# A recurrence's values spread by DMA, its key products on GpSimd, weights issued behind the first inputs

## What is computed

```
def step(s, inp):                      # s: (B, 32 heads, 8, 8)
    k_l, v_l, w_l, r_l = inp
    a = k_l[..., :, None] * v_l[..., None, :]
    out = einsum('bhs,bhst->bht', r_l, faaaa * a + s)
    s_new = a + w_l[..., None] * s
    return (s_new, out)
```

## Time and profile before

| | us |
|---|---|
| median of 3 runs | 1033.08 |
| the profiled execution, whole | 1040.02 |
| its span, first to last instruction | 1037.9 |
| TensorE busy | 960.1 (92%) |
| VectorE busy | 742.7 (72%) |
| ScalarE busy | 572.7 (55%) |
| GpSimd busy | 543.3 (52%) |
| mean granted TensorE clock | 0.979 |

### The profile page before, as it was taken

One profiled execution on the slowest core, in us unless ns is written; L12 is line 12 of the kernel. 1 busy time (PEld: TensorE's weight loads), 2 busy tenths in 40 slices (PEclk: granted clock), 3 DMA queues, 4 the chain that ended last, 5 costly groups with the idle time before them and its releaser, 6 DMA issues.

```text
span 1037.9 us, 27518 instructions
## 1 busy us (share of the span) xinstructions
PE 960.1 (92%) x10944; PEld 764.5 (74%) x10944; DVE 742.7 (72%) x1607; ACT 572.7 (55%) x1320; POOL 543.3 (52%) x662
## 2 busy tenths in 40 slices
PE   6979999989789999889999999998998999899997
PEld 4657886856567877668887788776767777688885
DVE  1485566788997788973756765676889887986675
ACT  2489733432333755667746587644545452575573
POOL 2364353574754456774426633555565664675341
PEclk9999999998897999999999999999999999999999
DMA  9601111000001001020101001101001000000001
GB/s 346 274 2 30 29 29 28 2 1 2 2 1 33 1 2 28 3 65 2 29 27 34 27 2 29 29 2 27 2 1 29 14 1 2 13 9 6 13 2 43
DMA packets 28589, 31.71 MB, mean 31 GB/s; under 512 B 14736, under 2 KB 25264, under 8 KB 27824
## 3 DMA queue, kind: packets, MB, share of 16 engines
q1 hardware_dynamic: 27440, 28.12, 8.4%
q10 hardware_dynamic: 1024, 1.85, 0.5%
HBM read 27.86 MB, written 2.10 MB: 29 GB/s over the span
## 4 chain that ended last, share of the span: by engine, by line
PE 53%; DVE 19%; DVEq 9%; issue 7%; ACT 5%; POOL 4%; POOLq 2%; DMA 1%; ACTq 0%; SPq 0%
PE bank L494 8%; PE bank L506 7%; PE bank L378 6%; PE bank L366 5%; PE bank L399 5%; PE bank L391 3%; DVE lane L1013 3%; DVEq L1016 3%; DVE bank L1009 2%; PE bank L457 2%; DVEq L886 2%; PE bank L481 2%; DVE lane L865 2%; PE bank L524 2%; PE bank L535 2%
## 5 line engine op out<-in xcount | busy, mean ns | idle before, releaser
L1420 POOL TENSOR_TENSOR lane<-lane 128x512 f32<-128x512 f32 x160 | 167.8, 1052 | 159.1 <-DVE lane L887 90.8
L1186 ACT COPY lane<-bank 128x512 f32<-128x512 f32 x232 | 132.0, 590 | 166.8 <-PE bank L366 103.9
L366 PE MATMUL bank<-ident,lane 128*128 128x128 f32 x896 | 131.9, 282 | 16.4 <-POOL lane L1420 4.5
L366 PEld LDWEIGHTS bank<-ident,lane 128*128 128x128 f32 x896 | 102.7, 143 | 42.8 <-issue 14.8
L1492 POOL TENSOR_TENSOR lane<-lane 128x512 f32<-128x512 f32 x64 | 81.3, 1271 | 70.1 <-DVE lane L1013 69.8
L1013 DVE TENSOR_TENSOR_SCAN lane<-lane,bank 128x256 f32<-128x256 f32 x128 | 80.9, 674 | 5.0 <-issue 0.4
L1205 ACT ACTIVATE lane<-lane 128x512 f32<-128x512 f32 x96 | 60.3, 633 | 28.9 <-DVE lane L865 28.5
L1154 ACT ACTIVATE lane<-lane 128x256 f32<-128x256 f32 x96 | 52.3, 594 | 42.4 <-POOL lane L1405 42.0
L885 DVE TENSOR_REDUCE lane<-lane 128x8 f32<-128x512 f32 x96 | 64.8, 675 | 12.1 <-ACT lane L1205 11.7
L1217 ACT ACTIVATE lane<-bank,vecs 128x256 f32<-128x256 f32 x128 | 51.9, 477 | 36.6 <-PE bank L494 36.3
L1168 ACT ACTIVATE lane<-bank,vecs 128x256 f32<-128x256 f32 x112 | 55.3, 550 | 22.9 <-PE bank L366 22.5
(11 more groups left out here) (161 smaller groups left out, 2243.4 us busy)
## 6 DMA issues: line engine op xcount, KB each, us to landing
lane<-in_inT SPq DMA_DIRECT2D x16, 256.0 KB, 4.5
lane<-in_x SPq DMA_DIRECT2D x16, 256.0 KB, 2.9
w_d<-in_w_d SPq DMA_DIRECT2D x1, 3072.0 KB, 25.1
w_am<-in_w_am SPq DMA_DIRECT2D x1, 2048.0 KB, 15.5
lane<-in_inT SPq DMA_DIRECT2D x16, 128.0 KB, 3.0
lane<-in_ctx SPq DMA_DIRECT2D x8, 256.0 KB, 2.9
out_x<-lane SPq DMA_DIRECT2D x8, 256.0 KB, 2.2
w_c<-in_w_c SPq DMA_DIRECT2D x1, 1792.0 KB, 20.3
```

Source lines behind the costliest of these rows:

```text
L366: ins = pe.transpose(t[:, i * P:(i + 1) * P], src, ident[:, :])
L1186: s.copy(out, src).then_inc(bk.free_sem(key), 1)
L1420: p.tensor_tensor(q, q, den.unsqueeze(2).to_broadcast([P, n, 512 // n]), ALU.mult).then_inc(sig["normal"].sem, 1)
```

## The change

- TensorE's `spread_values` and the `spread` matrix are gone. SP stores the values of a group, shifted by one token, to a DRAM tile (256 KB), and after it has landed reads it back in four halves, each with four DMAs that put 16 rows on 128 partitions (8 copies). The halves are four SBUF tiles (`halves`), the first and the last at the same place.
- The product with k moves from VectorE (PSUM) to GpSimd (SBUF, in place), as `product(u)`; for every second unit it first copies s0 into the first column. `read(u)` is the old product with r. The order of both within a group is `PRODUCTS`, 16 steps where there were 8.
- The scans read and write SBUF in place.
- The context and cross mask of a group are loaded after its `y`, since their place now holds values.
- At the start SP issues inputs and masks before `am`, and `b` only once all four x have landed; `c` and `d` follow after group 1's second x load.
- Counters are merged (`rk`, `rs` into `products`; `bias` into `x_bias`; `ctx_loaded`, `mask3_loaded` into `l3_loaded`). All `ORDER` strings and `BANKS` are new. Not shown: the strings for VectorE and ScalarE, `BANKS`, the renamed waits, the constants.

```diff
-BIAS = {"self": 1, "cross": 2, "m": 3}
+BIAS = {"self": 3, "cross": 4, "m": 5}
...
+SPREADS = 4
+
+PRODUCTS = ["rk"] + [name + str(u) for name, u in zip("kkrkrkrkrkrrkkrr", (0, 1, 0, 2, 1, 3, 2, 4, 3, 5, 4, 5, 6, 7, 6, 7))]
+PRODUCT = {name: k + 1 for k, name in enumerate(PRODUCTS)}
...
+    ("l3_loaded", 2, 16), ("stored", 1, 16),
+    ("v_stored", 1, 16), ("v_spread_a", 2, 16 * SPREADS), ("v_spread_b", 2, 16 * SPREADS),
...
 ORDER = {
     "PE": (
+        "P0000101011122122233303032010210012102120120010120100121213120100000000003100211131110312233032110323100130100"
+        "20212230213023222132222011131211323132013333333233032022123023023120133301330230131002302020131112201111310200"
+        "30320223000322012210131101332130101300300330121302022020200212020003002300121311332310131002313212021203213120"
+        "31011012110212101203113133032313122222222303201012200112102131200333113233000102110033320322301333210020310312"
+        "12112230211010300330110013003231001023231322320211202311201113201011203131203230233010233223023122212222232110"
+        "31311321121320333033323333332220122030323210333031032130133100202201302111211101321030032020320002302012031211"
+        "33130120001110303013231030020220002301203222333003201231311312100103003102121212231211120131112112223202222222"
+        "032233223232112313333213323333333133300031031220123213233131313"
...
     "POOL": (
+        "001112100020232121020013011P2102301230210333030201013020003000000001012200113001103111211211111113232211212122"
+        "00233222233222232233301223330313333033031010033320201002110112313011000000300221122231020022333330113221112113"
+        "31222322121123210302302323033233333301011100020232010120011110301213131322210022223310202033310130203300203000"
+        "00011020310201010310111121111113213122312210212103223322223222233233202233331133303333001300023321000102102101"
+        "1331001100000302121322102002332323331213321101111323232122221122333322323030321033320222131133313"
...
     "SP": (
+        "0110232033P031221P01PP02000013111102222323323310312200030011131122022313330020001131112222132033332031231023"
...
+                self.halves = [self.at(at, 4 * G, S).rearrange("p (e b) t -> p e b t", e=4) for at in (4672, 512, 1536, 4672)]
+                self.shifted_v = self.arena[:, 4111:4623]
...
+                self.s0 = self.arena[:, 5696:5760].rearrange("p (m e b) -> p m e b", m=CT, e=SH)
+                self.v_d = nc.dram_tensor(f"lane{i}_v", (P, CT * T), F32, kind="Internal").ap()
+
+            def state(self, m, i):
+
+                return self.halves[2 * m + i // 2][:, 2 * (i % 2):2 * (i % 2) + 2, :, :]
...
-            def spread_values(m, i0):
-                t = [pe_open(pe, (g, "spread", m, i)) for i in (i0, i0 + 1)]
-                for e in range(2):
-                    for n in range(2):
-                        q = slice(32 * (i0 + n), 32 * (i0 + n) + 32)
-                        pe.matmul(tokens(t[n][:, e * T:(e + 1) * T])[:, :, 1:S], spread[q, e, :], tokens(L.bv[q, m, :])[:, :, 0:S - 1],
-                                  start=True, stop=True)
-                for n in range(2):
-                    i = i0 + n
-                    q = slice(32 * i, 32 * i + 2 * G)
-                    pe.transpose(t[n][:, :].rearrange("p (e t) -> p e t", t=S)[:, :, 0], L.s0T[q, m, :], ident[q, 32 * i:32 * i + 2 * G]).then_inc(
-                        bk.full_sem((g, "spread", m, i)), 1)
-
...
-                pe.wait_ge(sig["rs"].sem, sig["rs"].at(g, 4 * m + 4))
+                pe.wait_ge(sig["products"].sem, sig["products"].at(g, PRODUCT["r" + str(4 * m + 3)]))
...
-                st = L.state[:, 2 * i:2 * i + 2, :, :]
-                kv = bk.tile(key)[:, :].rearrange("p (e b t) -> p e b t", e=2, b=G)
-                v.tensor_tensor(kv, kv, L.bk[:, m, :, 0:S].unsqueeze(1).to_broadcast([P, 2, G, S]), ALU.mult)
-                v.drain()
+                st = L.state(m, i)
                 w = L.wS[:, m, :, :].rearrange("p b t -> p (b t)")
                 for e in range(2):
-                    ins = v.tensor_tensor_scan(st[:, e, :, :].rearrange("p b t -> p (b t)"), w, bk.tile(key)[:, e * T:(e + 1) * T], 0.0,
-                                               ALU.mult, ALU.add)
+                    kv = st[:, e, :, :].rearrange("p b t -> p (b t)")
+                    ins = v.tensor_tensor_scan(kv, w, kv, 0.0, ALU.mult, ALU.add)
                 ins.then_inc(sig["scanned"].sem, 1)
-                v.drain().then_inc(bk.free_sem(key), 1)
 
             for m in range(CT):
...
+            def product(u):
+                m, i = u // 4, u % 4
+                if u % 2 == 0:
+                    landed = sig["v_spread_a" if i == 0 else "v_spread_b"]
+                    p.wait_ge(landed.sem, landed.at(g, m + 1))
+                    if u == 0:
+                        p.wait_ge(sig["bd_loaded"].sem, sig["bd_loaded"].at(g, 1))
+                    p.tensor_copy(L.halves[u // 2][:, :, :, 0], L.s0[:, m, 2 * i:2 * i + 4, :])
+                st = L.state(m, i)
+                p.tensor_tensor(st[:, :, :, 1:S], st[:, :, :, 1:S], L.bk[:, m, :, 1:S].unsqueeze(1).to_broadcast([P, 2, G, S - 1]),
+                                ALU.mult).then_inc(sig["products"].sem, 1)
+
+            def read(u):
+                m = u // 4
+                p.wait_ge(sig["scanned"].sem, sig["scanned"].at(g, u + 1))
+                st = L.state(m, u % 4).rearrange("p e b t -> p e (b t)")
+                p.tensor_tensor(st, st, L.br[:, m, :].unsqueeze(1).to_broadcast([P, 2, T]), ALU.mult).then_inc(sig["products"].sem, 1)
+
+            for name in PRODUCTS[1:]:
+                if name[0] == "k":
+                    product(int(name[1]))
+                else:
+                    read(int(name[1]))
+                yield
 
...
+        def sp_spread(sp, g, half):
+            L = lane(g)
+            sig = L.sig
+            for e in range(4):
+                k = 4 * (half % 2) + e
+                sp.dma_start(flat(L.halves[half][:, e, :, :]), L.v_d[16 * k:16 * k + 16, T * (half // 2):T * (half // 2) + T].unsqueeze(0).to_broadcast([SH, 16, T]).rearrange("s h c -> s h c")).then_inc(sig["v_spread_b" if half % 2 else "v_spread_a"].sem, 16)
...
-                sp.dma_start(L.s0T, a["s0T"][g].rearrange("p (m k) -> p m k", m=CT)).then_inc(sig["bd_loaded"].sem, 16)
+                sp.dma_start(L.s0, a["s0"][g].rearrange("p (m e b) -> p m e b", m=CT, e=SH)).then_inc(sig["bd_loaded"].sem, 16)
+                yield
+                for name in ("maa_k", "maa_v"):
+                    sp.wait_ge(bk.free_sem((g, "proj", name)), bk.taken_at((g, "proj", name)))
+                sp.dma_start(L.v_d, L.shifted_v).then_inc(sig["v_stored"].sem, 16)
+                yield
+                sp.wait_ge(sig["v_stored"].sem, sig["v_stored"].at(g))
+                sp_spread(sp, g, 0)
+                yield
+                sp.wait_ge(bk.full_sem((g, "proj", "maa_g")), bk.full_at((g, "proj", "maa_g")))
+                sp_spread(sp, g, 1)
+                yield
+                sp.wait_ge(sig["v_spread_a"].sem, sig["v_spread_a"].at(g, 1))
+                sp_spread(sp, g, 2)
+                yield
+                sp.wait_ge(sig["summed"].sem, sig["summed"].at(g))
+                sp.wait_ge(sig["v_spread_b"].sem, sig["v_spread_b"].at(g, 1))
+                sp_spread(sp, g, 3)
+                yield
+                sp.wait_ge(bk.full_sem((g, "y")), bk.full_at((g, "y")))
                 for ct in range(CT):
...
+            for g in range(NL):
+                sp.wait_ge(lane(g).sig["x_loaded"].sem, lane(g).sig["x_loaded"].at(g, 1))
             sp.dma_start(wt["b"][:, :], a["w_b"]).then_inc(load["b"].sem, 16)
```

128 lines of the change are left out of this document (43 added, 85 removed).

## The result

The changed kernel takes 1069.2 us (median of 4 runs, 1067.8 to 1072.3) where the kernel before takes 1033.9 beside it (1033.0 to 1037.4): 1.032 times as long, 95% interval 1.029 to 1.036. 1071 had been forecast. Its profiled execution has a span of 1066.6 us, 28.7 above that of before. The profiled execution of before is a long one of its kernel (1040.0 against a median of 1033.9), so the 35 us between the medians are the figure to go by, and the stretches of the earlier trace rows are a few us longer in all than in a typical execution.

A forecast was written before the change was run, and what follows sets the result against it. TensorE, busy 92%, was taken as the bound, with VectorE and TensorE waiting for each other in the first recurrence stretch. 729 us outside the recurrence stretches plus 172 + 175 gave 1076, less 5 on the median: 1071 us, range 1005 to 1108.

The forecast's parts named there:

- TensorE, 34 us less work, busy near 925: Whole span: dropping the 32 `spread_values` calls takes 34 us off TensorE; in the recurrence stretches it is busy 60 to 70%.
- VectorE, 44.5 us less: Whole span: 64 key products of 0.695 us, 44.5 us in all, and 64 drains leave VectorE.
- GpSimd, 631 us, lists of 127 and 130: GpSimd rises from 543 to 631 us; its own work in the two recurrence stretches adds up to 127 and 130 us.
- The turns of the scans: Recurrence stretches: scans with two SBUF operands exclude GpSimd's work, some 0.55 us each, 35 us per stretch.
- rival 3: Recurrence stretches: half of the turns fall on moments when GpSimd waits anyway; stretches 150 + 155, median 1029 us; chance 0.10.
- The remainder of the stretches: Recurrence stretches: 10 us for VectorE's other two-operand instructions, nothing for GpSimd's waits; 172 and 175 us with list and turns.
- Rival 1: Recurrence stretches: scans don't exclude GpSimd; stretches 135 + 140, median 999 us, up to 1020; chance 0.22.
- The landings at 0, bounds 0 to 10: Recurrence stretches: waits for the value halves spread by DMA cost 0, at most 10 us per stretch, as other lanes' steps cover them.
- rival 2: Recurrence: late landings stop all four lanes, 91 us more, about 1162; sign: over 20 us of GpSimd's DMA waits; chance 0.08.
- The SP waits put at 0: SP's order: eight more waits per group in five more steps cost 0, since the loads behind them are needed much later.
- The start, 5 us gained: Before the first bonus product: masks ahead of the large weights let softmax run beside the projections, 5 us gained (0 to 10).
- Between and after: Stretches between and after the recurrences: TensorE work of 341 and 215 us plus idle time of 16 and 13.

## Why the prediction was right, step by step

**TensorE, 34 us less work, busy near 925.** The instructions went (x10944 to x10624), but TensorE was busy 944.6. Outside the recurrence stretches it needed 676.7 where I had counted 686; in them 127.9 and 140.0 instead of 109 and 116, so that it was busy 74 and 80% there and not 60 to 70: records at the lower clock are longer (the bonus product's take 379 ns by the median and up to 767), and the granted clock fell to 0.86. That TensorE fell idle in both stretches was right. That its relief alone would be worth 34 us was wrong: 24 us less busy moved the time by 3 to 5.

**VectorE, 44.5 us less.** True of the products, and more than eaten by the scans: 55.9 us of turns.

**GpSimd, 631 us, lists of 127 and 130.** 643.9 busy. Without the turns the lists were 122 and 126: the key product takes 1.18 us, not the 1.27 that I took from L1492. It has 504 elements for each partition and L1492 has 512, which doesn't explain it; the mixes of the earlier trace rows, which have 512, take 1.18 too.

**The turns of the scans.** Their existence was forecast from L962 alone and held: maximum 1745 ns, median 772. The median well above 675 that I had named fits, the maximum near 1.9 about. The Trainium skill's rule ("GPSIMD Engine Reference", section "Key points": contention with VectorE instructions that have two SBUF inputs) agrees with the traces in both directions: one operand moved to SBUF brought scans of up to 1690 ns into the kernel before, where 690 had been the longest, and one operand less took them out of the changed kernel (687 at most). One reading of the earlier trace rows was loose: L1420 ends 0.37 us late, not by the 0.51 that L962 had left. The other pair says the same (0.54 late of 0.69): some 0.15 us of the later instruction is not held up. The step that failed is the price: 35 us per stretch, on the argument that each turn adds to GpSimd's list. VectorE grew by 32.6 us and GpSimd by 9.1, but the stretch by 16.3, since part of the turns fell into time in which the other engine, or the same one, would have waited (the sums leave no other place for it; single turns were not followed). That was rival 3's mechanism, and it held for half of the price.

**The remainder of the stretches.** I had 10 us for other two-operand instructions and nothing for GpSimd's waits, on the ground that such waits were in the sum already. They weren't: without any turns of scans the stretches were 155.4 and 159.9, 33 us above GpSimd's busy time in each. The terms as measured for the first: 122 for the list, 33 waits, 16 turns, 171; as forecast: 127, 10 and 35, 172. Rival 1's 135 and 140 were wrong in the same place, so even scans that never took turns would have given 1038 and not 999.

**The landings at 0, bounds 0 to 10.** Right, in the new order: without any transfer the time is the same. The sign that I had named for rival 2, more than 20 us of GpSimd's waits for DMA, was met at 20.9 and misled: a wait in the list says who came last, not what the time would be without that wait. Where the transfers were made later (one DMA per half), the cover was gone at once, for 12 us. The SP waits put at 0 stayed without a visible price.

**The start, 5 us gained.** The first stretch is 147.9 with 130 us of my step times in it, against 147.4 with 127: some 3 us, and in the kernel before 2. **Between and after** I had 357 and 228 (341 + 16 and 215 + 13), measured 345.9 and 225.3; with the start's 147.9 that is 719 against my 729. (The working once gives 12 to 19 us of idle time for these three stretches; the rows have 11 to 19, and the sum uses the 11.)

**How much of the closeness is luck.** The direction and its reason were forecast, and they held. The size came out by luck, in two places. Each stretch is met within 1 us (171.7 and 175.8 for 172 and 175) by the two errors above. And the sum on the span was 1076, 9 us more than the 1066.6 measured; it came back to 1071 by the 5 us taken off for the median, which only reflected that the profiled execution of before was a long one. Of the changed kernel the median, 1069.2, lies 2.6 above the profiled span.

**What costs 35 us, then.** Scans that take turns: without them the changed kernel equals the kernel before (1.001). That doesn't make them the only term. Without the key products on GpSimd the changed kernel is 1.5% faster than before, without both 2.5%, and what TensorE's relief gives in return is small. The change paid with SBUF operands and GpSimd time for something that the recurrence was not waiting for. No form tried here beats the kernel before clearly while doing its whole work; the new start alone comes nearest (0.9985).

## What to carry to other kernels

Before moving work off an engine that is busy 92%, find out in which stretches that work lies and whether the engine sets their pace; a run with the work left out prices it, and here 24 us were worth 3 to 5. Moving an operand from PSUM to SBUF isn't free when the other engine works in SBUF beside it: look in the trace for instructions with two SBUF operands and a long maximum, and count how many more there will be. And test a long wait by taking away what it waits for before you believe its length: 20.9 us of waits for landings were worth nothing.

## What was unexpected in the hardware

- Turns are not paid in full: 32.6 us on VectorE and 9.1 on GpSimd for 16.3 us of elapsed time in one stretch.
- GpSimd's products of nearly the same shape have two durations, 1.27 (reads L1483) and 1.18 us (mixes L1460 and key products L1476), whatever the kernel; the cause was not sought.
- One DMA of 512 KB in place of four of 128 KB, with fewer packets (35114 instead of 47147 in all) and a quarter of the issues for the spreads, was waited for longer: 37.4 us against 20.9. (The store before it went out in two parts as well, which alone put the first spread of group 0 back by 2 us.)
